# A GRU's input state: stored after normalising, or rebuilt by its reader from the tile before normalising

## The reference

```python
x = x + L0_gnn(layernorm(x), src, dst)        # three GraphSAGE layers
x = x + L0_ffn(layernorm(x))                  # 8 experts, top 2, gelu
x = x + L1_gnn(layernorm(x), edge_type, src, dst)   # relations and a GRU
x = x + L1_ffn(layernorm(x))                  # 16 experts, top 2, relu
```

```python
msg = h[src] + relvectors[edge_type]
red = segment_sum(msg, dst)
gi, gh = red @ w_ih.T + b_ih, h @ w_hh.T + b_hh
r, z = sigmoid(gi_r + gh_r), sigmoid(gi_z + gh_z)
n = tanh(gi_n + r * gh_n)
x = x + (1 - z) * n + z * h
```

## Time and profile before

| | us |
|---|---|
| median of 3 runs | 1700.25 (1699.76 to 1701.4) |
| the profiled execution, its own time | 1701.26 |
| its span in the profile | 1698.8 |
| PE busy | 1499.6 |
| DVE busy | 846.4 |
| ACT busy | 486.1 |
| POOL busy | 338.3 |
| relate's tile loop, from its first load to the first sum of the second half | 1004.45 to 1080.60 |
| gru, from its first instruction | 1181.08 |

### The profile page before, as it was taken

The page is one execution under the profiler, slowest core; times in us unless marked ns, Lnnn a source line. Parts: engine busy times, 40 slices in busy tenths (PEclk is TensorE's granted clock), DMA queues, the critical chain, the costliest instruction groups (busy, mean ns, idle before and its releaser), DMA issues. The chain is left out here.

```text
span 1698.8 us, 33464 instructions
## 1 busy us (share of the span) xinstructions
PE 1499.6 (88%) x8652; PEld 1054.0 (62%) x8652; DVE 846.4 (50%) x2425; ACT 486.1 (29%) x1258; POOL 338.3 (20%) x393
## 2 busy tenths in 40 slices
PE   3796799999999999985999957898999849999977
PEld 3685654458444855544999942344566639999864
DVE  6897753233333467775222238511588762232227
ACT  2565320013000311112454433100223314444434
POOL 3000220003000310003555530000001224555430
PEclk9555899999999999996999979999999859999989
DMA  4000331124112332222233347401222244332435
GB/s 127 0 0 1 94 96 49 49 78 133 53 47 59 124 97 83 84 75 100 93 98 118 118 126 238 137 25 53 76 65 65 93 166 158 121 119 94 143 99 181
DMA packets 134635, 158.57 MB, mean 93 GB/s; under 512 B 16929, under 2 KB 119698, under 8 KB 134258
## 3 DMA queue, kind: packets, MB, share of 16 engines
q1 hardware_dynamic: 122642, 125.59, 23.7%
q0 software_dynamic: 11840, 32.12, 6.2%
q10 hardware_dynamic: 96, 0.20, 0.0%
HBM read 103.12 MB, written 57.93 MB: 95 GB/s over the span
## 5 line engine op out<-in xcount | busy, mean ns | idle before, releaser
L898 PE MATMUL layer_ps<-parts,counts 128*128 128x512 f16 x1875 | 409.1, 379 | 1.2 <-issue 0.6
L898 PEld LDWEIGHTS layer_ps<-parts,counts 128*128 (+1 forms) x1875 | 183.3, 98 | 217.8 <-issue 2.8
L1444 ACT ACTIVATE experts_hT<-experts_ps_h,experts_b_col 128x128 f32<-128x128 f32 x456 | 160.9, 368 | 102.3 <-PE experts_ps_h L1419 80.9
L1427 PE MATMUL experts_ps_y<-experts_rows,experts_hT 128*128 128x256 f32 x688 | 163.9, 381 | 0.8 <-ACT experts_hT L1444 0.2
L1382 POOL DMA_INDIRECT chosen<-experts_y,experts_row x116 | 114.6, 988 | 151.4 <-issue 130.0
L1427 PEld LDWEIGHTS experts_ps_y<-experts_rows,experts_hT 128*128 128x128 f32 x688 | 124.2, 190 | 16.1 <-ACT experts_hT L1444 2.5
L799 POOL TENSOR_TENSOR parts<-layer_rest,gru_rows 128x256 f32 (+2 forms) x75 | 54.4, 726 | 392.5 <-DVE layer_rest L774 392.5
L1371 POOL DMA_INDIRECT experts_fetched<-tokens,experts_index x120 | 116.1, 967 | 75.1 <-issue 46.6
L960 DVE COPY layer_total<-layer_ps 128x256 f32<-128x256 f32 x75 | 31.8, 425 | 183.6 <-PE layer_ps L898 180.7
L1419 PEld LDWEIGHTS experts_ps_h<-experts_xT,experts_rows 128*128 128x128 f32 x976 | 120.1, 194 | 4.0 <-DVE experts_xT L1460 0.9
L1419 PE MATMUL experts_ps_h<-experts_xT,experts_rows 128*128 128x128 f32 x976 | 120.6, 277 | 0.5 <-DVE experts_xT L1460 0.5
(11 more groups left out here) (316 smaller groups left out, 2089.1 us busy)
## 6 DMA issues: line engine op xcount, KB each, us to landing
experts_rows<-in_L_ffn_w SPq DMA_DIRECT2D x32, 512.0 KB, 5.1
gru_rows<-x SPq DMA_DIRECT2D x75, 128.0 KB, 2.2
own<-layer_own SPq DMA_DIRECT2D x75, 128.0 KB, 1.7
layer_own_in<-own SPq DMA_DIRECT2D x75, 128.0 KB, 2.1
h<-layer_out SPq DMA_DIRECT2D x50, 128.0 KB, 1.7
gru_rows<-h SPq DMA_DIRECT2D x50, 128.0 KB, 2.1
gru_rows<-chosen SPq DMA_DIRECT2D x50, 128.0 KB, 2.4
combine_y<-chosen SPq DMA_DIRECT2D x50, 128.0 KB, 2.4
```

The costliest lines, as they stand in the source:

```text
L898: last = nc.tensor.matmul(ps[b][:], cst.counts[:, s, bass.ds(t * P, P)], parts[:, s, :], start=s == 0, stop=s == NT - 1)
L1427: last = nc.tensor.matmul(ps_y[:, 0:D], hT[:, c, :], down[b][:, c, :], start=c == 0, stop=c == KH - 1)
L1444: nc.scalar.activation(hT[:, c, :], ps_h[c][:, 0:P], function, bias=b1_col[:, bass.ds(e * KH + c, 1)]).then_inc(hT_ready, 1)
```

## The change

`hn` is no longer made, stored or loaded.

- In relate DVE leaves out L1645. POOL makes from a tile's mean and reciprocal four 128x1 values: mean * inverse, that times -2048 (`low_bias`), and, kept for all tiles in two resident tiles, `state_inverse` and `state_bias` = -(mean * inverse). It waits for the reciprocal and for the lower part of tile t-2, and drains behind the first product.
- ACT's upper part is an Identity activation of the mixed tile with scale and bias by 128x1 pointers, and waits for POOL. DVE's remainder is mixed tile * inverse - upper part, a scalar_tensor_tensor; ACT's lower part adds the bias -2048 * mean * inverse.
- SP stores only the mixed tile, which has four buffers now. DVE waits for the store of tile t-4 in place of t-2.
- In gru SP loads `red` and x2; "the unit" of the state is ACT: an Identity activation of the loaded x2 tile (`normalise_state`) writes the state into the buffer that was loaded before. ACT does it for tile t+3 behind the tanh of tile t, and for tiles 0, 1 and 2 before its first copy. PE's turn and DVE's z * state wait for `state_ready`.
- To make room, `inv_deg`, the small statistics of the layers and `not_before` of the routing lie in tiles that are there already.

The core of the diff (uses of `not_before` and the signature of `gru` are left out):

```diff
@@ -1015,13 +1015,14 @@
-        room.hT, room.rest, room.own, room.small = pair("hT", [P, KD, P]), pair("rest", [P, D]), pair("own", [P, D]), pair("small", [P, 10])
+        room.hT, room.rest, room.own = pair("hT", [P, KD, P]), pair("rest", [P, D]), pair("own", [P, D])
...
+        room.small = [odd[:, 64 + b * 10:74 + b * 10] for b in range(2)]
@@ -1103,14 +1104,15 @@
-        not_before = sb("not_before", [P, P])
...
-        at_place = [sb(f"at_place{c}", [P, P, NT], F16) for c in range(2)]
+        places = [sb(f"at_place{c}", [P, P * NT], F16) for c in range(2)]
+        at_place = [a[:].rearrange("p (a t) -> p a t", t=NT) for a in places]
+        not_before = places[1][:, 0:2 * P].bitcast(F32)
@@ -1504,20 +1506,20 @@
-        mixed, out, small = pair("mixed", [P, D]), pair("out", [P, D]), pair("small", [P, 10])
-        hn, rest = pair("hn", [P, D]), pair("rest", [P, D])
+        mixed, out, small = pair("mixed", [P, D]), [sb(f"out{b}", [P, D]) for b in range(B)], pair("small", [P, 10])
+        rest, low_bias, offset = pair("rest", [P, D]), pair("low_bias", [P, 1]), pair("offset", [P, 1])
+        nothing, minus_low = sb("nothing", [P, 1]), sb("minus_low", [P, 1])
...
-        stored, hn_stored, red_stored = ([sem(f"{n}{b}") for b in range(2)] for n in ("stored", "hn_stored", "red_stored"))
+        stored, red_stored = [sem(f"stored{b}") for b in range(B)], [sem(f"red_stored{b}") for b in range(2)]
...
-        normed, hi_ready, rest_ready, lo_ready = sem("normed"), sem("hi_ready"), sem("rest_ready"), sem("lo_ready")
+        biased, hi_ready, rest_ready, lo_ready = sem("biased"), sem("hi_ready"), sem("rest_ready"), sem("lo_ready")
...
-        loop = lambda engine, step: tile_loop(engine, step, n=B, ahead=2, behind=2)
-        buffer = lambda k, b: (k * 2 + b // 2, b % 2)
+        loop = lambda engine, step: tile_loop(engine, step, n=B, ahead=2, behind=B)
@@ -1537,18 +1539,12 @@
-                def store_normed(u, b):
-                    sp.wait_ge(normed, u + 1)
-                    sp.dma_start(dr.hn[rows(u), :], hn[b % 2][:]).then_inc(hn_stored[b % 2], 16)
...
-                    sp.dma_start(dr.x2[rows(t), :], out[b % 2][:]).then_inc(stored[b % 2], 16)
-                    if not early(t - 1):
-                        store_normed(t - 1, b + 1)
+                    sp.dma_start(dr.x2[rows(t), :], out[b][:]).then_inc(stored[b], 16)
@@ -1558,17 +1554,33 @@
-                store_normed(NT - 1, NT - 1)
...
+                for b in range(B):
+                    sp.wait_ge(stored[b], 16 * uses(b, B))
...
-                    sp.wait_ge(stored[b], 16 * uses(b))
-                    sp.wait_ge(hn_stored[b], 16 * uses(b))
...
+                def bias_of(k, b):
+                    t, d = k * B + b, b % 2
+                    pool.wait_ge(inverted, t + 1)
+                    if not early(t - 2):
+                        pool.wait_ge(lo_ready, t - 1)
+                    nc.gpsimd.tensor_tensor(offset[d][:], small[d][:, 6:7], small[d][:, 9:10], ALU.mult)
+                    pool.drain()
+                    nc.gpsimd.tensor_tensor(low_bias[d][:], offset[d][:], minus_low[:], ALU.mult)
+                    nc.gpsimd.tensor_tensor(cst.state_inverse[:, bass.ds(t, 1)], small[d][:, 9:10], cst.ones[:, 0:1], ALU.mult)
+                    nc.gpsimd.tensor_tensor(cst.state_bias[:, bass.ds(t, 1)], nothing[:], offset[d][:],
+                                            ALU.subtract).then_inc(biased, 1)
...
+                pool.drain()
+                nc.gpsimd.memset(nothing[:], 0.0)
+                nc.gpsimd.memset(minus_low[:], -LO_SCALE)
+                pool.drain()
+                tile_loop(pool, bias_of, n=B, behind=B)
@@ -1605,20 +1617,21 @@
-                    act.wait_ge(normed, u + 1)
+                    act.wait_ge(biased, u + 1)
...
-                    nc.scalar.copy(tile_of(parts, u)[live, 0:D], hn[b % 2][live, :]).then_inc(hi_ready, 1)
+                    nc.scalar.activation(tile_of(parts, u)[live, 0:D], out[b % B][live, :], ACT.Identity,
+                                         scale=small[b % 2][live, 9:10], bias=cst.state_bias[live, bass.ds(u, 1)]).then_inc(hi_ready, 1)
...
-                    nc.scalar.activation(tile_of(parts, u)[live, D:2 * D], rest[b % 2][live, :], ACT.Copy,
-                                         scale=LO_SCALE).then_inc(lo_ready, 1)
+                    nc.scalar.activation(tile_of(parts, u)[live, D:2 * D], rest[b % 2][live, :], ACT.Identity,
+                                         scale=LO_SCALE, bias=low_bias[b % 2][live, :]).then_inc(lo_ready, 1)
...
-                        split(t - 1, b + 1)
+                        split(t - 1, (b - 1) % B)
@@ -1639,12 +1652,6 @@
-                def norm_of(u, use, b):
-                    if not early(u - 2):
-                        dve.wait_ge(hn_stored[b], use * 16)
-                    nc.vector.tensor_scalar(hn[b][:], out[b][:], small[b][:, 6:7], small[b][:, 9:10], ALU.subtract,
-                                            ALU.mult).then_inc(normed, 1)
@@ -1653,44 +1660,38 @@
                     dve.wait_ge(hi_ready, u + 1)
                     if not early(u - 2):
                         dve.wait_ge(lo_ready, u - 1)
-                    nc.vector.tensor_tensor(rest[b][:], hn[b][:], tile_of(parts, u)[:, 0:D], ALU.subtract).then_inc(rest_ready, 1)
+                    nc.vector.scalar_tensor_tensor(rest[b % 2][:], out[b][:], small[b % 2][:, 9:10], tile_of(parts, u)[:, 0:D],
+                                                   ALU.mult, ALU.subtract).then_inc(rest_ready, 1)
                 def step(k, b):
                     t = k * B + b
-                    use, d = buffer(k, b)
+                    d, before_d = b % 2, (b - 1) % 2
                     behind = not early(t - 1)
-                    before_use, before_d = buffer(k, b - 1) if b > 0 else buffer(k - 1, B - 1)
                     dve.wait_ge(got[b], k * 48 + 48)
                     nc.vector.scalar_tensor_tensor(mixed[d][:], y[b][0], plan.weight[0][:, bass.ds(t, 1)], x[b],
                                                    ALU.mult, ALU.add).then_inc(begun, 1)
                     if behind:
                         inverse_of(t - 1, before_d)
+                    if not early(t - B):
+                        dve.wait_ge(stored[b], k * 16)
+                    dve.wait_ge(begun, t + 1)
+                    nc.vector.scalar_tensor_tensor(out[b][:], y[b][1], plan.weight[1][:, bass.ds(t, 1)], mixed[d][:],
+                                                   ALU.mult, ALU.add).then_inc(taken, 1)
+                    dve.wait_ge(taken, t + 1)
+                    nc.vector.bn_stats(small[d][:, 0:6], out[b][:])
                     if not early(t - 2):
-                        dve.wait_ge(stored[d], use * 16)
-                    dve.wait_ge(begun, t + 1)
-                    nc.vector.scalar_tensor_tensor(out[d][:], y[b][1], plan.weight[1][:, bass.ds(t, 1)], mixed[d][:],
-                                                   ALU.mult, ALU.add).then_inc(taken, 1)
-                    if behind:
-                        dve.wait_ge(inverted, t)
-                        norm_of(t - 1, before_use, before_d)
-                    dve.wait_ge(taken, t + 1)
-                    nc.vector.bn_stats(small[d][:, 0:6], out[d][:])
-                    if not early(t - 2):
-                        remain(t - 2, d)
+                        remain(t - 2, (b - 2) % B)
                     dve.drain()
                     nc.vector.bn_aggr(small[d][:, 6:8], small[d][:, 0:6]).then_inc(var_ready, 1)
                 loop(dve, step)
-                u, use, d = NT - 1, (NT - 1) // 2, (NT - 1) % 2
+                u, d = NT - 1, (NT - 1) % 2
                 inverse_of(u, d)
-                dve.drain()
-                norm_of(u, use, d)
-                remain(NT - 2, 1 - d)
-                dve.drain()
+                remain(NT - 2, (NT - 2) % B)
                 dve.wait_ge(cleared, 1)
-                remain(NT - 1, d)
+                remain(NT - 1, (NT - 1) % B)
                 dve.wait_ge(v_hi_ready, 1)
                 dve.wait_ge(v_loaded, 16)
                 nc.vector.tensor_tensor(rest[0][rels, :], vectors[rels, :], parts[rels, NT - 1, 0:D],
@@ -1700,7 +1701,7 @@
-                        dve.wait_ge(stored[b], 16 * uses(b))
+                        dve.wait_ge(stored[b], 16 * uses(b, B))
@@ -1893,6 +1894,7 @@
+        state_ready = sem("state_ready")
@@ -1920,7 +1922,6 @@
-                    sp.dma_start(x[b][1][:], states[rows(t), :]).then_inc(loaded[b], 16)
@@ -1948,7 +1949,8 @@
-                    pe.wait_ge(loaded[b], loads * 48)
+                    pe.wait_ge(loaded[b], loads * 32)
+                    pe.wait_ge(state_ready, loads * B - (B - 1 - b))
@@ -2015,6 +2017,11 @@
+                def normalise_state(t, b, loads):
+                    act.wait_ge(loaded[b], loads * 32)
```

(15 more changed lines are left out.)

6 lines of the change are left out of this document (3 added, 3 removed).

## The result

The changed kernel took 1707.36 us, the median of 6 executions (1706.25 to 1711.42); beside it the kernel before took 1699.77 (1698.23 to 1701.4). The ratio is 1.0047, 95% interval [1.0036, 1.0057]: slower by about 8 us, clear of no change. Forecast were 1705.3 us and a range of 1694.5 to 1712. The profiled execution has an own time of 1708.46 and a span of 1706.3, 7.5 more than before's 1698.8.

A forecast was written before the change was run, and what follows sets the result against it. PE was busy 88% of the span, but relate's loop was bound by a 2.42 us DVE-ACT ring. Terms -6.6 + 7.9 + 0.7 + 3.0 = +5.0 on 1701.26 gave 1706.3, 1705.3 us at the median; range 1694.5 to 1712.

The forecast's parts named there:

- Part 1: Relate's loop: with the normalised state's stores gone and four mixed-tile buffers, DVE's waits for stores vanish, -6.6 us.
- only one kind goes: Relate's loop: the bound where waits for just one of the two kinds of store vanish, -5.9 us.
- Rival D: Relate: DMA load, not the stores, stalled DVE; part returns as waits for loads, up to +3 us; no chance given.
- Parts 2 and 3: Relate's DVE work and ACT forms: ring by way of DVE 2.37 us a tile, 0.05 under today's.
- Part 4: Relate: POOL's new chain is a second ring; its first instruction lets the mixed tile pass, 24 x 0.33 = +7.9 us.
- rival B: Relate and GRU: POOL's instructions overlap, never last; GRU Identity +1.0; sum -6.5, 1693.8 us; decides at chain 0.82; chance 0.22.
- Forecast: Main case: in relate only POOL's first instruction collides, with the mixed tile, 0.33 a tile; 1705.3 us; chance 0.45.
- rival C: Relate: POOL collides with both mixed tile and remainder, 24 x 0.73 = 17.5; sum +14.6, 1714.9 us; chance 0.08.
- Tail +0.7: End of relate's loop: the last tile's upper part comes by way of POOL, 1.8 us for about 1.1, +0.7.
- Part 5: GRU: ACT's added Identity delays the copy of the turned input, +3.0 us in all, bounds +1.0 and +5.0.
- two-tile argument: GRU loop: the copy comes 0.36 late against the tile two before, so 0.18 us in each tile.
- +0.5 for the stage's start: GRU's start: an Identity stands between the load's landing and the transpose, less one load ahead, +0.5 us.

The follow-up runs named there:

- Experiment 3: The kernel before with only the four buffers for the mixed tile, the normalised state still made and stored: 1700.62 us against 1699.89, ratio 1.0005.
- kernel 11: The kernel before with four mixed-tile buffers and without the normalised state's store; result not the reference's, only stretches compared: relate's 24 gaps between reciprocals 57.8 us.
- experiment 9: The changed kernel with POOL's three drains in this stage replaced by semaphores: 1697.16 us against 1700.65 for the kernel before, ratio 0.9978.
- Experiment 6: The kernel before with the GRU's weight loads issued ahead of the last store of the normalised state: 1696.32 us against 1698.11, ratio 0.9987.

## Why the prediction was right, and where it wasn't

The direction came out, and the time lies in the range: +5.0 was forecast, the medians moved by 7.6 and the profiled spans, from the first load on, by 4.7. That the sum fits so well is partly luck, by two missed terms that nearly cancel. For relate's loop parts 1 and 4 together said +1.3, and it grew by 5.9, 4.0 of it through a late start of POOL; for the sums there was no term, and they fell by 5.1.

- **Part 1, -6.6: the size right, the reason half wrong.** The waits are gone, and leaving the write out is worth 7.4 us in the loop. But the step argued with the buffer that comes back after four tiles, and bounded the case "only one kind goes" at -5.9. Experiment 3 shows that bound to be wrong: with the second store still there, its waits take the place of the first's, and the gain is 0.2. The lower bound should have been zero, "what is late next" being the other store. Rival D's worry, loads in place of stores, didn't come true: the only wait for a load is the first, 10.8 us.
- **Parts 2 and 3: right.** (The 0.40 said to lie between the normalising instruction's start and the next is 0.32 in rows 4; the term, from 0.72 to 0.52, doesn't use it.) Bn_stats starts 0.52 behind the mixed tile (1033.07 to 1033.59), the remainder takes 0.468; upper part 0.60 for 0.58, lower part 0.492 for 0.49. Identity wanted no table of its own: ACT loads tables 14 times in either kernel.
- **Part 4, +7.9: the mechanism right, the size too small, the start missing.** The chain, estimated at 0.87 from first start to last end, is 0.85 in the tile shown above (1036.06 to 1036.91, the next reciprocal after 2.49). With no DVE instruction beside it, in tile 0, it is 0.80 (1017.17 to 1017.97), which is the mark below which the prediction said it would be wrong and under the 0.82 of rival B. So the chain's own length didn't carry the term, the collisions did. POOL's first instruction is held in 20 of the 25 tiles. The 23 gaps behind the first average 2.83, predicted 2.75; against the 2.43 of kernel 11 that is 0.40 a tile for 0.33, since in 19 of the 25 tiles one of the later instructions meets the remainder and ends with it. Forecast and rival C weren't alternatives: which collisions happen goes tile by tile. The Trainium skill's rule (SBUF — State Buffer, sections "SBUF: two separate sides" and "Who interferes with whom": the first to start has the shared ports for its whole length, the other blocks fully) agrees with the trace where POOL comes second: 0.48 started 0.05 behind the mixed tile, 0.19 started before it. Where DVE comes second the trace shows no full block: with POOL 0.04 ahead the mixed tile takes its usual 0.485.
- **Part 4 left out the first drain.** The term was "24 tiles by 0.33"; the rows had POOL drains with a gap of 0.15, and I took that price for each. The first one of this stage cost 9.3 us, 4 of them on the path. In the kernel before this stage had no drain in front of work, but the one at the end of its block took 9.78 us at that same place (experiment 9): the price stood in the trace of before, in a line where nothing waited for it.
- **Tail +0.7:** measured +0.9.
- **Part 5, +3.0: right in kind, somewhat large.** PE's first periods alternate between 5.6 and 6.0 as the two-tile argument says; the 23 periods behind the first took 2.3 us more than before. ACT in one tile (tanh, Identity, copy), and PE's matmuls behind it:

```profile
1238.04 0.42 ACT L2054 ACTIVATE gru_new<-gru_cand 128x256 f32<-128x256 f32 x1 [2.73 <-DVE gru_cand L2115]
1238.37 0.58 ACT L2022 ACTIVATE gru_x<-gru_before,state_bias,state_inverse 128x256 f32<-128x256 f32 x1
1238.86 0.56 ACT L2027 COPY gru_xT<-gru_ps_t 128x512 f32<-128x512 f32 x1
```

```profile
1239.50 3.68 PE L1968 MATMUL gru_ps_g<-gru_wT,gru_xT 128*128 128x512 f32 x8
```

  The copy is 0.82 behind the tanh where it was 0.33, and the matmuls follow its end by 0.08. The +0.5 for the stage's start didn't show (19.6 us from its first turned weight to the second tile's matmuls before, 19.4 after).
- **Part 6, 0:** nothing in the traces speaks against it; the first load came between 1006.9 and 1010.6 with either layout.
- **Missing: the sums, -5.1.** The step "SP issues four DMAs a tile for five" counted the queue in the loop, not at its end, where one store held back 1.5 MB of weights ahead of the sums' stores. Experiment 6 shows it on the kernel before, at about half the size, and kernels 3 and 11 fit its line.

What stays open: why this drain takes 9.3 us. Since the drain before it POOL has issued 112 indirect transfers (their rows are picked by an index table), nearly all in the expert stage, which ends without a drain, so a price for those transfers is a natural reading. The traces speak against a price for each of them: in the very first stage the gap at a drain behind ten such transfers is 1.65 to 2.40 us, and behind the second expert stage, with 128 of them and again no drain in between, the first drain takes 1.45 us. In the kernel before:

```profile
L1736 POOLq DRAIN  x1: 1454/1454/1454, 1643.3 to 1643.3; - x1
```

Nor is it an end that is waited for: in experiment 9 the drain stands 69 us behind the last transfer and is as long. What sets the two stages apart here was not tested. Also open is the +0.9 behind the GRU, within what single executions differ by.

## What to carry to other kernels

Small work on POOL is cheap in duration and dear in position: if it sits between two DVE instructions on a ring, its order of start against them decides, so form everything that doesn't need the last value early, signal after the first instruction, and keep drains out of the chain (a semaphore raised by the instruction itself took 0.08 in place of 0.15, and left a drain of 9.3 us to a place where nothing waits for it). Before a first drain is put ahead of work, look in the trace for what the drain at the end of that block costs now. When a store is removed, look at what stood behind its wait in the queue after the loop, not only in it. When two buffers stall in turn, count a gain only for relieving both.

## What the runs showed of the hardware that was not expected

- The first drain on POOL behind the first expert stage (112 indirect transfers): a gap of 9.31 to 9.33 us in the seven kernels that had it ahead of work, 0.15 for later ones. Where the stage has no other, the drain at the end of its block is the first and lasts 9.75 to 9.81 us, even 64 to 69 us behind the last transfer. The first one behind the second expert stage (128 transfers): 1.45 to 1.59 us.
- POOL's 128x1 tensor_tensor: 0.19 alone, starts 0.14 apart when independent. Started 0.05 to 0.29 behind a DVE instruction of 128x256 that reads two SBUF operands, it ends 0.05 behind that one's end, whenever it started (0.24 to 0.48 long). Started 0.04 to 0.05 before one or, in kernel 9, 0.03 behind it, it keeps 0.19. DVE's mixed tile takes 0.485 in either order; in kernel 9, with POOL 0.11 ahead and again 0.03 behind, the remainder takes 0.49 for 0.47.
- A memset moved between engines changed which of the two starts first in one gap in four, worth 0.5 to 0.6 us in each such gap.
